# Query, key and value projections as three float16 products, and an earlier place for the next tile's transposes

## What is computed

```python
h = _layernorm(x, axis=-1) * (1 + ca) + sa
Q = h @ Wq.T + bq;  K = h @ Wk.T + bk;  V = h @ Wv.T + bv
Q, K = _rope(Q, pos), _rope(K, pos)
scores = jnp.einsum('bhqd,bhkd->bhqk', Q, K) * scale      # causal mask
attn = jnp.einsum('bhqk,bhkd->bhqd', softmax(scores), V)
x = x + ga * (attn.transpose(0, 2, 1, 3).reshape(B, S, D) @ Wo.T + bo)
h = _layernorm(x, axis=-1) * (1 + cb) + sb
x = x + gb * ffn(h)      # routed: gelu(t @ w1[e] + b1[e]) @ w2[e] + b2[e]
```

## Time and profile before

| | us |
|---|---|
| median of 3 runs | 800.48 |
| lowest and highest run | 797.1 and 801.36 |
| span of the profiled execution, first to last instruction | 795.7 |

### The profile page before, as it was taken

One profiled execution on the slowest core, in us unless ns is written; L12 is line 12 of the kernel. 1 busy time (PEld: TensorE's weight loads), 2 busy tenths in 40 slices (PEclk: granted clock), 3 DMA queues, 4 the chain that ended last, 5 costly groups with the idle time before them and its releaser, 6 DMA issues. The chain is left out here.

```text
span 795.7 us, 20973 instructions
## 1 busy us (share of the span) xinstructions
PE 705.5 (89%) x7310; PEld 435.7 (55%) x7310; DVE 602.1 (76%) x1238; ACT 502.3 (63%) x1001; POOL 441.7 (56%) x577
## 2 busy tenths in 40 slices
PE   7868889999999999999999888674999999999993
PEld 5433444454554555445445443353777777777772
DVE  5767887988889889798898766347677777777774
ACT  1426778888888888888888888632444444444441
POOL 4403554777777877877877777823133434334321
PEclk8998999999999999999999999966999999999998
DMA  8105233244444734525535347358365655423000
GB/s 269 34 1 116 73 100 101 79 144 111 147 126 105 170 100 139 148 81 140 126 97 149 101 152 159 108 208 302 99 190 171 182 181 154 128 70 96 23 19 1
DMA packets 61364, 97.49 MB, mean 123 GB/s; under 512 B 8405, under 2 KB 42318, under 8 KB 60753
## 3 DMA queue, kind: packets, MB, share of 16 engines
q1 hardware_dynamic: 56272, 79.36, 33.9%
q0 software_dynamic: 4992, 16.79, 6.7%
HBM read 69.47 MB, written 34.51 MB: 131 GB/s over the span
## 5 line engine op out<-in xcount | busy, mean ns | idle before, releaser
L1115 DVE TENSOR_REDUCE row_max<-ps_max 128x2 f32<-128x768 f32 (+2 forms) x192 | 199.8, 1041 | 51.1 <-PE ps_max L652 51.0
L925 ACT ACTIVATE prob<-ps_sc 128x1024 f32<-128x1024 f32 (+1 forms) x192 | 169.2, 882 | 60.3 <-PE ps_sc L679 59.3
L1466 PE MATMUL ps_h<-tok_t,w_all 128*128 128x128 f16 x1872 | 156.5, 219 | 2.6 <-issue 2.0
L1466 PEld LDWEIGHTS ps_h<-tok_t,w_all 128*128 x1872 | 131.8, 98 | 44.4 <-issue 4.3
L433 POOL TENSOR_SCALAR_AFFINE_SELECT prob<-prob 128x512 f32<-128x512 f32 x128 | 82.2, 642 | 86.9 <-ACT prob L925 86.5
L1379 POOL DMA_INDIRECT slot_mem<-row_dram,token x39 | 46.2, 1184 | 139.6 <-DVE y L1676 119.6
L1536 ACT ACTIVATE hid<-ps_h,b_t 128x128 f32<-128x128 f32 x312 | 89.1, 372 | 50.1 <-PE ps_h L1466 50.0
L1480 PE MATMUL ps_y<-w_all,hid_parts 128*128 x312 | 118.5, 381 | 2.0 <-DVE hid_parts L1651 1.9
L692 PE MATMUL ps_pv<-prob,v_sb 128*32 128x512 f32 (+3 forms) x1024 | 88.8, 442 | 0.3
L645 PE MATMUL ps_max<-k_t,q_t 64*128 64x512 f16 (+3 forms) x512 | 68.5, 304 | 22.9 <-DVE row_max L1115 22.1
L1482 PE MATMUL ps_y<-w_all,hid_parts 128*128 x312 | 85.0, 273 | 0.0
(11 more groups left out here) (257 smaller groups left out, 1345.6 us busy)
## 6 DMA issues: line engine op xcount, KB each, us to landing
raw<-w SPq DMA_DIRECT2D x64, 256.0 KB, 3.0
w_dram<-halves SPq DMA_DIRECT2D x64, 256.0 KB, 3.3
w_all<-w_dram SPq DMA_DIRECT2D x20, 512.0 KB, 4.0
row_dram<-rows SPq DMA_DIRECT2D x32, 256.0 KB, 3.4
w_all<-w_dram SPq DMA_DIRECT2D x3, 2048.0 KB, 12.8
mod_rows<-mods_dram SPq DMA_DIRECT2D x16, 256.0 KB, 6.8
row_dram<-mods_dram SPq DMA_DIRECT2D x32, 128.0 KB, 4.6
xs<-x SPq DMA_DIRECT2D x24, 128.0 KB, 3.4
```

The source lines that it names most:

```text
L925: nc.scalar.activation(p_kb[:, :, first * L:(first + n) * L], ps_sc[:, :, 0:n * L], ACT.Exp, scale=SCALE).then_inc(exp_done, 1)
L1115: nc.vector.tensor_reduce(dst, ps_max[:, :, 0:n * L].rearrange("p j (m l) -> p j m l", m=n), AX.X, ALU.max).then_inc(max_done, 1)
L1466: last = mm(o, w[:, :, k, f, :][:, bass.ds(e, 1), :].rearrange("p e m -> p (e m)"), tok_t[:, j % 2, piece, k, :], start=(n == 0 and f % HF ...
```

## The change

Each of `h` and the three weights is split into two float16 parts, a high and a low one, and three of the four products are summed: high by high, high by low weight, low by high weight. The weights carry a factor of 64 (`W_SCALE`), taken back in the rotary tables and where the values are kept.

- ACT writes the high part of the weights where it wrote the float32 ones; three new DVE instructions write the low part.
- A new ACT step, `high_h`, writes the high part of `h_t` behind `keep_shift`, at the end of a unit's list.
- A new POOL step, `low_h`, writes the low part, first in the list of a unit.
- In shot 0 PE makes the four products with the high part of `h`, and in shot 1 the two with the low part.
- PE transposes the next tile's `xhat` between the output projection and the queries' transposes, not behind the keys' transposes. DVE's `normalise` moves from shot 4 to shot 3, behind `divide`, and `modulate` moves from the end of the list to the place behind `negated`, ahead of `keep_qt` and `row_statistics`.
- Two semaphores are merged with others, which changes no order.

```diff
@@ POOL, the step added and its places
+            def low_h(T):
+                pool.wait_ge(h_high, T + 1)
+                nc.gpsimd.tensor_tensor(h16[:, 1, :, :], h_t[:, :, :], h16[:, 0, :, :], ALU.subtract).then_inc(h_low, 1)
...
             for T in range(LEAD):
                 rotate(T)
+                low_h(T + 1)
                 if T + 2 <= LEAD:
                     rstd_of(T + 2)
 
             for U in range(NU):
                 T = U + LEAD
+                if U and T < NT:
+                    low_h(T)
                 if U >= QT - 1:
                     add_const(U - QT + 1)
@@ PE
+            def project_qk(T, part, ps, kept_before):
+                if part == 0:
+                    pe.wait_ge(h_high, T + 1)
                     ge(pe, qt_kept, kept_before)
                     mm(ps, ones3[:, :], bias3[:, 0:2 * D], start=True, stop=False)
-                last = mm(ps, h_t[:, k, :], w_qkv[:, k, 0:2 * D], start=False, stop=(k == KC - 1))
+                    for k in range(KC):
+                        for piece in range(2):
+                            mm(ps, h16[:, 0, k, :], w16[:, k, piece, 0:2 * D], start=False, stop=False)
+                else:
+                    pe.wait_ge(h_low, T + 1)
+                    for k in range(KC):
+                        last = mm(ps, h16[:, 1, k, :], w16[:, k, 0, 0:2 * D], start=False, stop=(k == KC - 1))
                     last.then_inc(qk_ps, 1)
...
-                    last = mm(ps[:, 0:D], h_t[:, k, :], w_qkv[:, k, 2 * D:3 * D], start=(k == 0), stop=(k == KC - 1))
+                    for part, piece in ((0, 0), (0, 1), (1, 0)):
+                        last = mm(ps[:, 0:D], h16[:, part, k, :], w16[:, k, piece, 2 * D:3 * D],
...
                     if s == 5:
                         if X >= 0:
                             project_out(X, ps_nd)
+                        if T + 1 < NT:
+                            if U == 0:
+                                pe.wait_ge(gates_kept, 1)
+                            x_transposes(T + 1, ps_nd, U)
                         if T < NT:
                             q_transposes(T, ps_b[:, :])
@@ ACT
+            def high_h(T):
+                act.wait_ge(ht_done, KC * T + KC)
+                nc.scalar.activation(h16[:, 0, :, :], h_t[:, :, :], ACT.Copy).then_inc(h_high, 1)
...
                 if V < NU:
                     keep_shift(V)
+                if T + 1 < NT:
+                    high_h(T + 1)
@@ DVE, ahead of the lead
             modulate(0, ps_pv)
+            for n, ps in enumerate((ps_sc[:, 0, :], ps_sc[:, 1, :], ps_max[:, 0, :])):
+                dve.wait_ge(wt_kept, n + 1)
+                nc.vector.scalar_tensor_tensor(out=w16[:, :, 1, n * D:(n + 1) * D], in0=ps.rearrange("p (i o) -> p i o", i=KC),
...
             statistics(1)
@@ DVE, in a unit
+                    if s == 3:
+                        if U:
+                            divide(U - 1)
                         if T + 1 < NT:
                             normalise(T + 1)
+                    if s == 4 and T < NT:
+                        lo_parts(T)
                 if V < NU:
                     negated(V)
+                if T + 1 < NT:
+                    modulate(T + 1, ps_nd)
                 if T < NT:
                     keep_qt(T, ps_b[:, :])
                 if X > 0:
                     row_statistics(X - 1)
```

More of the change, by code:

```diff
@@ L611, in project_v @@
                 for k in range(KC):
-                    last = mm(ps[:, 0:D], h_t[:, k, :], w_qkv[:, k, 2 * D:3 * D], start=(k == 0), stop=(k == KC - 1))
+                    for part, piece in ((0, 0), (0, 1), (1, 0)):
+                        last = mm(ps[:, 0:D], h16[:, part, k, :], w16[:, k, piece, 2 * D:3 * D],
+                                  start=(k == 0 and part == 0 and piece == 0), stop=(k == KC - 1 and part == 1))
                 last.then_inc(v_ps, 1)
@@ L752, in _ @@
             pe.wait_ge(bias_spread, 48)
-            pe.wait_ge(wt_kept, 3)
+            pe.wait_ge(wt_low, 3)
             for T in range(LEAD):
                 ps_q, ps_v = lead_banks(T)
-                for k in range(KC):
-                    project_qk(T, k, ps_q, T - 1)
+                for part in range(2):
+                    project_qk(T, part, ps_q, T - 1)
                 project_v(T, ps_v, T - 1)
@@ L801, in _ @@
                         logit_products(Z // QT - 1, ps_nd)
-                    if s < KC and T < NT:
+                    if s < 2 and T < NT:
                         project_qk(T, s, ps_b[:, :], T)
@@ L868, in _ @@
                 act.wait_ge(wt_ps, n + 1)
-                nc.scalar.activation(w_qkv[:, :, n * D:(n + 1) * D], ps.rearrange("p (i o) -> p i o", i=KC),
-                                     ACT.Copy).then_inc(wt_kept, 1)
+                nc.scalar.activation(w16[:, :, 0, n * D:(n + 1) * D], ps.rearrange("p (i o) -> p i o", i=KC),
+                                     ACT.Copy, scale=W_SCALE).then_inc(wt_kept, 1)
+            def high_h(T):
+                act.wait_ge(ht_done, KC * T + KC)
+                nc.scalar.activation(h16[:, 0, :, :], h_t[:, :, :], ACT.Copy).then_inc(h_high, 1)
+            act.wait_ge(rope_loaded, 32)
+            for table in (cos_t, sin_t):
+                nc.scalar.activation(table[:, :, :], table[:, :, :], ACT.Copy, scale=1.0 / W_SCALE).then_inc(rope_loaded, 1)
+            high_h(0)
             def keep_v(T, ps, after_unit=None):
@@ L878, in keep_v @@
                 nc.scalar.activation(v_sb[:, par, t, :, 0:DK], ps[:, 0:D].rearrange("p (h d) -> p h d", h=H),
-                                     ACT.Copy).then_inc(v_kept, 1)
+                                     ACT.Copy, scale=1.0 / W_SCALE).then_inc(v_kept, 1)
             def hi_parts(T):
@@ L1201, in _ @@
                         statistics(T + 1)
-                    if s == 3 and U:
-                        divide(U - 1)
-                    if s == 4:
-                        if T < NT:
-                            lo_parts(T)
+                    if s == 3:
+                        if U:
+                            divide(U - 1)
                         if T + 1 < NT:
                             normalise(T + 1)
+                    if s == 4 and T < NT:
+                        lo_parts(T)
                 if V < NU:
                     negated(V)
+                if T + 1 < NT:
+                    modulate(T + 1, ps_nd)
                 if T < NT:
@@ L1214, in _ @@
                     row_statistics(X - 1)
-                if T + 1 < NT:
-                    modulate(T + 1, ps_nd)
             def row_offset(Y):
```

38 lines of the change are left out of this document (19 added, 19 removed).

## The result

| | before | after |
|---|---|---|
| median of the runs, us | 799.21 (797.1 to 801.36) | 840.2 (838.32 to 840.97) |
| ratio to before, 95% interval | | 1.0522 (1.0495 to 1.0549) |
| span of the profiled execution, us | 795.7 | 839.1 |
| `rope` of unit 0, unit 5, unit 26 starts at, us | 65.82, 136.92, 437.89 | 70.51, 143.09, 480.70 |
| mean of the 21 units between, us | 14.33 | 16.08 |

The change costs 41 us on the medians and 43.4 us on the spans. The table splits the 43.4: 6.2 us ahead of unit 5's `rope`, 36.6 us in the 21 units to unit 26, 0.6 us behind it.

What follows compares the result with a forecast made beforehand. A ring of PE and DVE was taken to bound the kernel before, a new ring through POOL after: 795.7 + 37 + 0 = 832.7 us, plus 4.8 us to the median, 837.5 us; range 808 to 850 us.

Steps and rivals of the forecast that it cites:

- The sign: Whole kernel: slower, chance 0.87; within 0.5%, 0.03; faster by over 0.5%, 0.10.
- the main term: Units 6 to 26: 1.77 us more a unit, 21 times, 37 us.
- The ring: Units 6 to 26: DVE's row statistics, POOL's row work and low part, PE's second half, `rope`; 16.10 us a unit.
- the port meeting: Moved `normalise` meets POOL's `low_piece` on the shared SBUF ports and is held up, ending at R+5.99.
- Rival B: In the loop, POOL doesn't hold `normalise` up: 15.42 us a unit, 23 us more, 823 us; 18%.
- Ahead of unit 6: Lead and units 0 to 5: added steps and gains add up to nothing, give or take 3 us.
- the low part ahead of `rstd_of`: In the lead on POOL, ahead of the result `normalise` needs: 1 us in all, between 0 and 2.
- The offset to the median: Added to the profiled execution's span: the median of the runs lies 4.8 us above it.
- C: In the loop, row work and low part end before PE asks: some 12 us faster, 788 us; 10%.
- D: PE waits for the low part without feedback: `rope` 0.48 us late, 21 times, 10 us, 811 us; 10%.
- E: PE's clock falls through waiting, in one unit in three: 28 us more, 865 us; 7%.
- the old ring: PE and DVE in the loop, 14.33 us a unit before the change; said to be slack after it.

Runs made afterwards that it cites:

- e1_low_first: The changed kernel with POOL's low part moved to the end of the unit before, ahead of the row work; 808.45 us, ratio 1.0126 to before.
- e2_norm_late: The changed kernel with `normalise` back in shot 4, behind `lo_parts`; 819.36 us, ratio 1.0278 to before.
- e3_moves_only: The float32 kernel before with only the three moves (`xhat` transposes, `normalise`, `modulate`); 821.14 us, ratio 1.0267 to before.
- e9_lead: The changed kernel with two lead steps moved: `rstd_of` ahead of the low part, weights' low parts ahead of the first `modulate`; 835.81 us, ratio 1.046 to before.
- e8_tuned: e4_both with the lead of e9_lead and the gating of weights moved behind the last `low_piece`; 790.93 us, ratio 0.9881 to before.
- e11_tuned_moves_undone: e8_tuned with the transposes and `modulate` back in their places of before; 807.04 us, ratio 1.0111 to before.
- e4_both: The changed kernel with the edits of e1_low_first and e2_norm_late together; 799.17 us, ratio 1.0006 to before.

## Why the prediction was right, and where it was off

The sign, the mechanism and the size of the main term hold. The total, 837.5 against 840.2 us, looks better than the working was.

**The ring, step by step: right.** From R = 255.36, what was worked out and what the earlier trace rows became:

| step | said | measured |
|---|---|---|
| `normalise` ends | R+5.99 | R+5.99 (260.25 + 1.10) |
| `modulate` starts | R+9.03 | R+9.00 |
| row statistics end | R+11.10 | R+11.06 |
| low part starts | R+14.63 | R+14.59 |
| low part ends | R+15.36 | R+15.26 |
| low part's products start | R+15.42 | R+15.32 |
| next `rope` | R+16.10 | R+15.96, mean of 21 units 16.08 |

The low part took 0.67 us, not the 0.73 of `add_const`: an instruction with the same 128x256 elements that reads one operand and writes its result in float16 is a little shorter. The 21 units cost 36.6 us, said 37. e1_low_first showed that the ring through POOL is the cause, e2_norm_late that the port meeting lengthens it.

**The port meeting: right.** The open point was whether a `normalise` behind `low_piece` behaves like the one behind the mask in the earlier trace rows. It does: 1.10 us, and 0.40 us in e2_norm_late. Rival B falls. By the Trainium skill, page "SBUF — State Buffer", section "Who interferes with whom", where both engines want the pair of ports that they share, the one that starts first keeps the other out until it ends. The trace agrees: `normalise` takes 1.10 us behind L488 of the change and 1.09 us behind L481 in e3_moves_only, and ends 0.16 us behind L488.

**Ahead of unit 6: mis-sized.** This is the term that failed, said 0 give or take 3 us, measured +6.2 at unit 5's `rope`. Its parts: the first tile's `rope` comes 1.7 us later (20.93 against 19.27), the fifth tile's 5.5 us (47.37 against 41.84), unit 0's 4.7 us (70.51 against 65.82). Then unit 0 is 0.8 us shorter, which was foreseen; unit 3, to 128.57, is 1.5 us longer; units 1, 2 and 4 are 0.2 to 0.3 us longer each, where I had put a gain: the meeting costs 0.7 us, not the 0.2 that I gave it in these units, because they too are the ring of PE and DVE, with `normalise` in it. Largest is the lead, where I had given the low part ahead of `rstd_of` 1 us in all. The timeline of DVE and POOL in the lead:

```profile
26.23 0.41 DVE L1103 TENSOR_SCALAR xhat<-xs,mean_var,rstd 128x256 f32<-128x256 f32 x1 [2.13 <-POOL rstd L418]
...
25.02 0.67 POOL L423 TENSOR_TENSOR h<-h_t,h 128x256 f16<-128x256 f32 x1
25.65 0.55 POOL L418 TENSOR_TENSOR rstd<-var_eps,neg_half 128x1 f32<-128x1 f32 x1
```

DVE waits 2.13 us, 0.63 of them for the low part; the queueing is the same trap as in the loop, and it comes with each tile of the lead. The port meeting comes there too, once: the second tile's `normalise` starts 0.07 us behind the first tile's low part (18.80 and 18.73 us) and takes 1.14 us, 0.52 in before. The working also took the clock to be full. The windows of after, twice in the lead and once in unit 3:

```profile
28.00:34.00 6.00, 3.77 (x18) 1.45 (x16) 3.65 (x13) 2.48 (x4) 2.46 (x4) 0.68 0.13 38
34.00:40.00 6.00, 4.58 (x29) 2.35 (x27) 3.43 (x9) 2.05 (x4) 1.63 (x3) 0.75 0.00 0
...
120.00:126.00 6.00, 5.27 (x63) 3.43 (x63) 4.16 (x8) 4.33 (x8) 3.32 (x5) 0.72 0.49 155
```

and the first of these in before:

```profile
28.00:34.00 6.00, 5.53 (x32) 2.98 (x31) 4.72 (x14) 1.58 (x3) 1.93 (x3) 1.00 0.07 23
```

A mean of 0.72 is time at both levels, 1.2 and 2.4 GHz. The unit from 112.78 to 128.57 takes 15.79 us, against 14.26 before; in e9_lead, where the granted clock stays at 1.00 all through that unit (108.65 to 123.25 us), it takes 14.60.

**The offset to the median: an error that helped.** The sum gave 832.7 us for the profiled execution's span, and that was 839.1, so the working was 6.4 us short. I then added 4.8 us, by which the median of three runs lay above the span of before. With a fourth run of the kernel before its median is 3.5 us above that span (799.21 and 795.7), and after's median is 1.1 us above its own. 3.7 us of the 6.4 thus cancelled. The offset mixed two things: in every run on record the time is 1.8 to 2.0 us longer than that same run's span, which would put the profiled execution of before at about 797.6 us (an estimate), near its fastest run. The other 2.9 us are the distance of the median from that one execution, and say nothing of after's.

**The rivals.** C needs PE not to wait for POOL, and it waits 21 times. D had the wait without feedback, 14.8 us a unit; it is 16.08. E: in 100 us of the loop PE was busy for 80% and the granted clock stayed at 1.00, though PE waits in each unit. The granted clock fell once, ahead of unit 5 and where PE doesn't wait for POOL: in the unit from 112.78 us, 1.2 us longer than in e9_lead.

```profile
200.00:300.00 100.00, 79.73 (x904) 43.78 (x903) 81.73 (x159) 77.20 (x129) 72.38 (x97) 1.00 0.42 118
```

**What the prediction didn't see.** The moves alone cost 17 us in the 21 units, with float32 products as well (15.15 against 14.33), most of it through `normalise`. I had worked out the meeting as a part of POOL's ring, took the old ring to be slack, and gave it 0.2 us where there is no row work. It lengthens the old ring by 0.7 us: 13.72 us a unit in e2_norm_late's first units, 14.4 in the changed kernel's. Then, the negated maxima (L1154) meet POOL's mask in their delayed place and take 0.66 us, not 0.21. In this kernel that costs nothing, since `modulate` waits for PE's transposes to about the same time.

**What stays open.** What brings the phases of a lower granted clock on: they fall in other places in each kernel (in before none between 28 and 40 us, in e8_tuned some behind unit 26). No run here took them away by themselves, so their share of the time ahead of unit 0 isn't known. The time behind unit 26's `rope` is open too: 357.8 us in before, 358.4 in after, 360.8 in e1_low_first, 363.2 in e11_tuned_moves_undone, and no expectation counted on it.

## What to carry to other kernels

A small step added at the head of an engine's list inherits the tail of the list before it: read which instructions end last there, on what they wait, and whether that chain starts at the engine that will now wait. If it does, the cost is a ring, paid in every round, and the cure is the order (1.57 us a unit here for one moved instruction of 0.67 us), provided that what the step needs is ready there as early (14.23 against 14.93 us a unit with the early and the late `modulate`). Before a DVE instruction between SBUF tensors is moved, look at what POOL does at that time: 0.40 us became 1.10 us.

## What the hardware showed that was not expected

- A DVE instruction of 16 elements a partition (L1154, SBUF to SBUF) takes 0.21 us alone, 0.66 us behind a mask of POOL's, and 1.00 us behind POOL's L488. `normalise`, with 256 elements a partition, takes 1.10 us when it starts 0.22 us behind L488, as this one does. So the hold doesn't go with the size of the instruction that is held up.
- The two-input L1134 takes 0.41 us alone and 0.85 us in such a meeting. In e4_both POOL's own mask, started 0.25 us behind DVE's L1133, took 0.83 us in place of 0.64, which suggests that the hold goes both ways.
- Behind 72 us the granted clock of after fell once in the loop, from 122 us on, and stayed at 1.00 in units with longer waits. PE's busy share alone doesn't tell where it falls: PE was busy for 3.83 of the 6 us ahead of that fall, and for 3.75 of 6 us in a unit with PE's long wait, where it stayed.

```profile
116.00:122.00 6.00, 3.83 (x49) 1.60 (x48) 5.93 (x10) 4.43 (x8) 3.60 (x5) 1.00 0.32 104
157.00:163.00 6.00, 3.75 (x38) 1.85 (x38) 4.50 (x9) 3.61 (x5) 5.28 (x8) 1.00 0.05 16
```
